# More idle-time identity products on TensorE, and GpSimd's power in two halves

## The chip, the cores and the metric

One core of one Trainium2 chip. The metric is the device time of one execution in microseconds; shown are the median of three runs and one execution that was profiled. The engines are TensorE (PE in the rows; PEld is its weight load), VectorE (DVE), ScalarE (ACT), GpSimd (POOL) and SyncE (SP), which issues the DMAs. Each engine works through its own list of instructions and waits for the others by semaphores.

## The reference, cut to what matters

The input is 8 batches of 512 tokens with 128 features. Each batch goes through six blocks, each behind a layer norm without weights:

```python
x = L0_attn_x                                    # 8 x 512 x 128
x = x + 0.5 * _L0_ffn_ref(_layernorm(x), ...)    # low rank: U1, V1, gelu, U2, V2
x = x + _L0_attn_ref(_layernorm(x), ...)         # 16 heads of 8, causal softmax, a layer norm inside
x = x + 0.5 * _L0_ffn_ref(_layernorm(x), ...)
x = x + 0.5 * _L1_ffn_ref(_layernorm(x), ...)    # shared expert and 8 routed ones, top 2
x = x + _L1_attn_ref(_layernorm(x), ...)         # Taylor feature map, num / den
x = x + 0.5 * _L1_ffn_ref(_layernorm(x), ...)

def _layernorm(x, axis=-1, eps=1e-05):
    m = jnp.mean(x, axis=axis, keepdims=True)
    v = jnp.var(x, axis=axis, keepdims=True)
    return (x - m) / jnp.sqrt(v + eps)
```

## The kernel before

A batch lies in SBUF as 128 partitions x 4 tiles (NT) x 128 features. Its work is cut into two halves: A is the first three blocks (low rank, softmax attention, low rank), B the last three (experts, Taylor attention, experts). Two sides run at once, left and right, each with its own region of SBUF and four banks of PSUM. The left side does A for batch after batch (stream A1) and B of the last (B1); the right side does A of one batch (A2), and then B for the others (B2). So in the steady state A of one batch runs beside B of an earlier one, and one turn of that takes about 180 us.

Each half is a list of named steps (ORDER_A, ORDER_B), the same for all engines. `stat` and `centre` are the layer norm on VectorE; `norm` (A) and `split` (B) transpose its result on TensorE. `low`, `up0` and `down0` are the low-rank block, `qkv0`, `pad0`, `max`, `shift`, `exp`, `pv0`, `turn` and `out0` the softmax attention: `max` forms scores for the row maxima, `shift` transposes the maxima, `exp` forms the scores again with the shift in an extra row. In B, `router`, `gate` and `expert` are the experts, `qk1`, `v1`, `pad1`, `sq`, `den`, `recip`, `num`, `scale` and `out1` the Taylor attention: `recip` inverts the denominators on VectorE, and `scale` spreads the reciprocals over the partitions by a product on TensorE.

The order in which an engine takes steps of the two sides is written out by hand, one letter (L or R) for each step and engine, in LOOP. It is the same before and after. So an engine that waits for data of one side holds up the other side's steps behind it.

TensorE's results go through a ring of PSUM banks, three in A and two in B. `fill` waits until the bank's last user has read it. Behind `fill`, and ahead of the wait for the step's data, several steps call `warm` (L1170), which looks up the stream, the turn and the step in the table WARM (L156) and runs that many 128x128 products of the identity with itself into the bank, which the step then overwrites. In the rows these products are L1173, two instructions each (fp32). The table has 26 entries with 144 products.

The layer norm goes over three engines. `stat` on VectorE makes means and variances of the four tiles (L909, L912). `ln_scale` on GpSimd adds epsilon (L710) and takes the power -0.5 (L712), each for all four tiles at once (128x4 elements). `centre` on VectorE (L920) waits for the power and does the four tiles one after the other, and then the transposes on TensorE (L1181) may start. Other lines in the rows: L1225 is `down0` behind the gelu, L1260 and L1262 `max`, L1408 `scale` behind `recip` (L1135), L988 `pad0`.

Of the kernel before, what the change touches and what calls it, by code (L numbers as in the profile page):

```python
# [33 lines left out]
ALU = mybir.AluOpType  # L34
# [5 lines left out]
NT = S // P  # L40
# [29 lines left out]
def segment(kt, head, heads):  # L70

    if kt == 0:
        return head * S
    if kt == 1:
        return (heads + head) * S
    if kt == 3:
        return (heads + head) * S + WIDTH[1]
    return 2 * heads * S + head * WIDTH[2]
# [64 lines left out]
def turns_of(body):  # L144
# [10 lines left out]

WARM = {  # L156
# [7 lines left out]
}  # L164

LOOP = {
# [247 lines left out]
def build_program(nc, x, w, cst, out):  # L414
    ctx = ExitStack()
    with ctx:  # L416
        def sb(name, shape, dt=F32):
            return ctx.enter_context(nc.sbuf_tensor(name, shape, dt))
# [16 lines left out]
        neghalf = sb("neghalf", [P, NT])  # L435
# [34 lines left out]
        def attention_stream(name, side):  # L470

            h = stream(name, side)
            new = h.region.take
            h.T, h.per, h.lns = TA, PERA, 4
            h.ring, h.pv = h.banks[0:3], h.banks[3]
            h.lnT = new([P, S])
            h.probs = new([P, 2, COLS0])
            h.hid0 = h.probs[:, 1, 0:NF * S].rearrange("p (f s) -> p f s", f=NF)
            p16 = h.probs[:, 1, NF * S:].bitcast(F16)
            h.q0h, h.q0l, h.k0h, h.k0l = (p16[:, i * S:(i + 1) * S] for i in range(4))  # L480
            h.kall = p16[:, 4 * S:(4 + NG) * S].rearrange("p (g s) -> p g s", g=NG)
            h.low = h.probs[:, 1, NF * S:NF * S + S // 2].bitcast(F16)
            h.mixed = h.probs[:, 0, 8 * S:9 * S]
            h.staging = h.probs[:, 0, :]
            h.q0a = new([P, NG, S], F16)
            h.kpad0 = new([P, H0, S], F16)
            h.vaug = new([P, NT, H0, HD0 + 1])
            h.bmax, h.rmax = new([P, NU0 * NT]), new([P, NT, H0])
            h.offs = new([GH, NG, S], F16)
            h.oT = new([P, 2, S])  # L490
            h.rden = new([P, NG, NT, GH, 1])
            h.attn = new([P, NT, D])
            h.qk0_laid = [sem(f"qk0_laid{g}_{name}") for g in range(NG)]
            h.offs_laid = [sem(f"offs_laid{g}_{name}") for g in range(NG)]
            h.low_hi = sem(f"low_hi_{name}")
            (h.kpad0_ready, h.rmax_ready, h.masked0, h.pv0_done, h.oT_ready) = (
                 sem(f"kpad0_ready_{name}"), sem(f"rmax_ready_{name}"), sem(f"masked0_{name}"),
             sem(f"pv0_done_{name}"), sem(f"oT_ready_{name}"))
            return h
# [45 lines left out]
        A1, A2 = attention_stream("A1", 0), attention_stream("A2", 1)  # L545
        B1, B2 = taylor_stream("B1", 0), taylor_stream("B2", 1)
# [39 lines left out]
        def run(eng, fns, engine):  # L586

            steps(fns, 0, "all", engine)
# [15 lines left out]
        def drained(h, it, step, unit):  # L604

            u = h.T[step, unit]
            return it * (h.per.act if u.engine == "act" else h.per.dve) + u.count
# [86 lines left out]
        @block.gpsimd  # L694
        def _(pool):
            for h in (A1, A2):
                pool.memset(h.vaug[:, :, :, HD0:HD0 + 1], 1.0).then_inc(setup, 1)
            pool.memset(neghalf[:, :], -0.5).then_inc(setup, 1)
            pool.memset(epsilon[:, :], LN_EPS).then_inc(setup, 1)
            for k in range(GP):  # L700
                if k:
                    pool.memset(column[:, k, 0:k], 0.0)
                pool.memset(column[:, k, k + 1:32], 0.0)
                last = pool.memset(column[:, k, k:k + 1], 1.0)
            last.then_inc(setup, 1)
            pool.wait_ge(setup, SETUP)

            def ln_scale(h, it, k, step):
                pool.wait_ge(h.mv_ready, it * h.lns + k + 1)
                pool.tensor_tensor(h.vare[:, :], h.mv[:, :, 1], epsilon[:, :], ALU.add).then_inc(h.vare_ready, 1)  # L710
                pool.wait_ge(h.vare_ready, it * h.lns + k + 1)
                pool.tensor_tensor(h.rstd[:, :], h.vare[:, :], neghalf[:, :], ALU.pow).then_inc(h.rstd_ready, 1)  # L712

            def mask(buf, heads, kt, fill=0.0):

                step = {0: S, 1: S, 3: S, 2: WIDTH[2]}[kt]
                s0 = segment(kt, 0, heads)
                v = bass.AP(buf.tensor, buf.offset + s0, [list(buf.ap[0]), [step, heads], [1, P]])
                return pool.affine_select(out=v, in_=v, compare_op=ALU.is_ge, fill=fill, base=0,  # L719
                                          pattern=[[0, heads], [1, P]], channel_multiplier=-1)  # L720

            def exp(h, it, n, step):
                g, u = divmod(n, NU0)
                if u in COMPLETE0:
                    pool.wait_ge(h.act, drained(h, it, step, "s"))
                for kt in COMPLETE0.get(u, ()):
                    mask(h.probs[:, g % 2, :], GH, kt).then_inc(h.masked0, 1)

            def sq(h, it, n, step):
                p, u = divmod(n, NU1)  # L730
                if u in COMPLETE1:
                    k = p * NC + list(COMPLETE1).index(u)
                    pool.wait_ge(h.act, drained(h, it, step, "s"))
                    for kt in COMPLETE1[u]:
                        last = mask(h.wts[:, p % 2, :], 2, kt, -1.0)
                    last.then_inc(h.cut1, 1)
                    pool.wait_ge(h.cut1, it * NPAIR * NC + k + 1)
                    v = h.wts[:, p % 2, (u // 2 * 2) * S:(u + 1) * S]
                    pool.tensor_scalar(v, v, 1.0, 1.0, ALU.mult, ALU.add).then_inc(h.masked1, 1)  # L739

            run(pool, dict(stat=ln_scale, exp=exp, sq=sq), "pool")

# [118 lines left out]
        def _(dve):  # L862
            passed = Passed(dve)
# [51 lines left out]
            def centre(h, it, k, step):  # L915

                src = h.attn if h in (A1, A2) and k == 2 else h.x
                passed.wait_ge(h.rstd_ready, it * h.lns + k + 1)
                for t in range(NT):
                    last = dve.tensor_scalar(h.ln[:, t, :], src[:, t, :], h.mv[:, t, 0:1], h.rstd[:, t:t + 1],  # L920
                                             ALU.subtract, ALU.mult)
                last.then_inc(h.ln_ready, 1)
# [219 lines left out]
            def out1(h, it, n, step):  # L1142
                ps = full(passed, h, it, step, "y")
                if n:
                    passed.wait_ge(h.dve, drained(h, it, f"out1 {n - 1}", "y"))
                dve.tensor_tensor(h.x[:, :, :].rearrange("p t d -> p (t d)"), ps[:, :],
                                  h.x[:, :, :].rearrange("p t d -> p (t d)"), ALU.add).then_inc(h.dve, 1)

            fns = dict(stat=stat, centre=centre, split=split, low=low, down0=down0, qkv0=qkv0, pad0=pad0, pv0=pv0, turn=turn,
                       out0=out0, take=take, route=route, gate=gate, expert=expert, qk1=qk1, pad1=pad1, recip=recip,  # L1150
                       scale=scale, out1=out1)
# [323 lines left out]
```

## Time and profile before

| what | before |
|---|---|
| median of 3 runs | 1472.24 us (1469.65 to 1478.45) |
| profiled execution, its own time | 1475.7 us |
| its span, first to last instruction | 1474.0 us |
| TensorE busy | 1260.9 us |
| VectorE busy | 950.3 us |
| ScalarE busy | 724.7 us |
| GpSimd busy | 420.0 us |
| mean granted clock of TensorE | 0.953 |

A row of the timeline has start, length, engine, line, operation, output and inputs, count, and in brackets the idle time of the engine just before it and what ended that.
### The profile page before, as it was taken

How to read it: one execution, taken by the hardware profiler on the slowest of the kernel's cores; microseconds unless marked ns; L12 is line 12 of the kernel's file. 1: busy time of each engine (PE TensorE's matmuls, PEld its weight loads, DVE VectorE, ACT ScalarE, POOL GpSimd, SP SyncE). 2: the span in 40 equal slices, each digit the busy share in tenths (PEclk: the TensorE clock that was granted, in tenths of full speed). 3: DMA queues.
4: the chain of work that ended last, by engine and by line, in shares of the span. 5: the costliest groups of instructions: out<-in, count | busy, mean ns of one | idle time of the engine just before them, and what ended most of it. 6: DMA issues, size and time to landing. Idle time of an engine off the chain costs nothing. (4 is left out here: it accounts for less than half of the span.)

```text
span 1474.0 us, 27223 instructions
## 1 busy us (share of the span) xinstructions
PE 1260.9 (86%) x10352; PEld 733.0 (50%) x10352; DVE 950.3 (64%) x2923; ACT 724.7 (49%) x1245; POOL 420.0 (28%) x707
## 2 busy tenths in 40 slices
PE   5598778988788887998789987888888988889998
PEld 3254454446544465444554445544555434653456
DVE  6986487446983479634896448863488645874267
ACT  3166436644366444664346543565434654456543
POOL 1023102640026400263003630035300362016730
PEclk9799899999999999999999999899998999999999
DMA  3100001000010000100101000010010100011000
GB/s 118 43 2 1 8 22 44 1 8 16 8 52 1 8 22 9 44 1 8 29 2 45 1 8 23 4 48 1 8 30 1 44 2 1 1 51 44 2 1 15
DMA packets 37203, 28.78 MB, mean 20 GB/s; under 512 B 7960, under 2 KB 36304, under 8 KB 37072
## 3 DMA queue, kind: packets, MB, share of 16 engines
q1 hardware_dynamic: 37072, 27.04, 6.8%
q8 instruction: 82, 1.34, 0.4%
q14 instruction: 49, 0.40, 0.1%
HBM read 5.90 MB, written 2.10 MB: 5 GB/s over the span
## 5 line engine op out<-in xcount | busy, mean ns | idle before, releaser
L998 DVE TENSOR_REDUCE left<-bank 128x4 f32<-128x512 f32 x280 | 184.5, 682 | 28.5 <-PE bank L1262 26.7
L849 ACT ACTIVATE right<-bank 128x512 f32<-128x512 f32 x280 | 158.4, 596 | 89.0 <-PE bank L1372 80.3
L805 ACT ACTIVATE left<-bank 128x512 f32<-128x512 f32 x280 | 160.1, 598 | 82.8 <-PE bank L1283 81.3
L719 POOL TENSOR_SCALAR_AFFINE_SELECT left<-left 128x512 f32<-128x512 f32 (+1 forms) x144 | 82.8, 591 | 338.8 <-ACT left L805 303.3
L1196 PE MATMUL bank<-right,pairs 128*128 128x512 f16 x588 | 161.9, 398 | 11.9 <-DVE right L1077 5.8
L739 POOL TENSOR_SCALAR right<-right 128x1024 f32<-128x1024 f32 x168 | 153.0, 911 | 14.7
L1260 PE MATMUL bank<-left 128*128 128x512 f16 (+1 forms) x448 | 120.8, 319 | 34.5 <-DVE left L998 19.6
L719 POOL TENSOR_SCALAR_AFFINE_SELECT right<-right 128x256 f32<-128x256 f32 (+1 forms) x240 | 99.6, 427 | 161.0 <-ACT right L849 150.9
L1098 DVE SCALAR_TENSOR_TENSOR right<-bank,right 128x128 f32<-128x128 f32 x448 | 125.8, 342 | 11.8 <-PE bank L1348 6.9
L1398 PE MATMUL bank<-right 128*32 128x256 f32 (+3 forms) x1792 | 133.1, 435 | 0.0
L1348 PE MATMUL bank<-ew,right 128*128 128x128 f32 x896 | 120.5, 278 | 8.8 <-DVE right L1087 6.2
L1348 PEld LDWEIGHTS bank<-ew,right 128*128 128x128 f32 x896 | 114.1, 191 | 27.6 <-DVE right L1087 12.9
L1283 PE MATMUL bank<-left 128*128 128x512 f16 (+1 forms) x448 | 104.8, 307 | 23.5 <-DVE left L998 17.9
L824 ACT ACTIVATE right<-bank 128x512 f32<-128x512 f32 x112 | 66.1, 597 | 108.9 <-PE bank L1196 108.1
L710 POOL TENSOR_TENSOR right<-right,epsilon 128x4 f32<-128x4 f32 x25 | 5.4, 215 | 376.8 <-DVE right L912 376.8
L1372 PE MATMUL bank<-right 96*128 96x512 f16 x448 | 99.9, 307 | 4.3 <-ACT right L849 3.0
L1262 PE MATMUL bank<-negmask,identb 128*128 128x128 bf16 x512 | 100.1, 229 | 0.0
L1196 PEld LDWEIGHTS bank<-right,pairs 128*128 128x128 f16 x588 | 53.3, 102 | 74.2 <-DVE right L1108 12.4
L1398 PEld LDWEIGHTS bank<-right 128*32 128x32 f32 x1792 | 53.9, 109 | 64.8 <-issue 61.3
L1260 PEld LDWEIGHTS bank<-left 128*128 128x128 f16 x448 | 45.6, 102 | 76.2 <-DVE left L998 25.1
L1385 PE MATMUL bank<-right,column 128*32 128x256 f32 (+3 forms) x896 | 75.8, 448 | 1.2 <-POOL right L739 1.1
L1015 DVE COPY left<-bank 128x512 f32<-128x512 f32 x28 | 19.3, 689 | 84.4 <-PE bank L1294 84.4
(276 smaller groups left out, 2254.6 us busy)
## 6 DMA issues: line engine op xcount, KB each, us to landing
right<-right SPq DMA_DIRECT2D x168, 64.0 KB, 2.0
left<-left SPq DMA_DIRECT2D x168, 32.0 KB, 1.8
left<-x_dram SPq DMA_DIRECT2D x7, 256.0 KB, 2.8
out_dram<-right SPq DMA_DIRECT2D x7, 256.0 KB, 2.3
left<-left SPq DMA_DIRECT2D x24, 64.0 KB, 2.0
right<-right SPq DMA_DIRECT2D x24, 32.0 KB, 1.9
wo<-wo_dram SPq DMA_DIRECT2D x1, 512.0 KB, 3.6
ew<-ew_dram SPq DMA_DIRECT2D x1, 512.0 KB, 4.7
```

The lines of the kernel that those rows point to most:

```text
L719: return pool.affine_select(out=v, in_=v, compare_op=ALU.is_ge, fill=fill, base=0, pattern=[[0, heads], [1, P]], channel_multiplier=-1)
L739: pool.tensor_scalar(v, v, 1.0, 1.0, ALU.mult, ALU.add).then_inc(h.masked1, 1)
L805: act.activation(h.probs[:, g % 2, u * S:(u + 1) * S], ps[:, :], ACT.Exp).then_inc(h.act, 1)
L849: act.activation(h.wts[:, p % 2, u * S:(u + 1) * S], ps[:, :], ACT.Square, bias=1.0, scale=FEAT ** -0.5).then_inc(h.act, 1)
L998: dve.tensor_reduce(h.bmax[:, u * NT:(u + 1) * NT], ps[:, :].rearrange("p (b k) -> p b k", k=P), AX.X, ALU.max).then_inc(h.dve, 1)
L1098: last = dve.scalar_tensor_tensor(out=dst[:, t, :], in0=ps[:, t * P:(t + 1) * P], scalar=h.comb[:, t, e:e + 1], in1=h.acc[:, t, :], op0=AL ...
L1196: done = mm(out, left, right, start=first, stop=last)
L1260: mm(ps[:, c0:c0 + n_keys], h.q0a[:, g, qt * P:(qt + 1) * P], h.kpad0[:, g * GH + j, 0:n_keys], start=True, stop=False)
L1262: last = mm(ps[:, c0 + n_keys - P:c0 + n_keys], identb[:, :], negmask[:, :], start=False, stop=True)
L1283: last = mm(ps[:, c0:c0 + WIDTH[kt]], h.kpad0[:, g * GH + j, kt * P:(kt + 1) * P], h.q0a[:, g, kt * P:S], start=True, stop=True)
L1348: last = mm(ps[:, t * P:(t + 1) * P], h.hexp[:, e % 2, t * P:(t + 1) * P], ew2[:, e, :], start=True, stop=True)
L1398: last = mm(h.num[HD1 * j + c:HD1 * j + c + 32, kt * P:S], h.v1[:, kt, hd * HD1 + c:hd * HD1 + c + 32], h.wts[:, p % 2, c0:c0 + WIDTH[kt]] ...
```

## The change

Two things change. The table WARM has 63 entries with 401 products instead of 26 with 144: three entries grow (`norm 0` and `max 0` of A1's turn 1, `split 0` of B2's turn 5), and 37 are new. And `ln_scale` takes the power in two instructions of two tiles each, with one count of the semaphore behind each; `centre` waits for the first half ahead of tile 0 and for the second ahead of tile 2.

```diff
 WARM = {
     ("A1", 0, "up0 1"): 6, ("A2", 0, "down0 0"): 8, ("A1", 0, "low 1"): 6, ("A2", 0, "out0"): 4,
-    ("A1", 0, "down0 2"): 4, ("A1", 1, "norm 0"): 12, ("A1", 1, "low 0"): 4, ("A2", 0, "down0 3"): 4,
-    ("A1", 1, "max 0"): 12, ("B2", 0, "split 2"): 2, ("B2", 0, "router 1"): 6, ("A1", 2, "exp 0"): 2,
+    ("A1", 0, "down0 2"): 4, ("A1", 1, "norm 0"): 19, ("A1", 1, "low 0"): 4, ("A2", 0, "down0 3"): 4,
+    ("A1", 1, "max 0"): 28, ("B2", 0, "split 2"): 2, ("B2", 0, "router 1"): 6, ("A1", 2, "exp 0"): 2,
     ("B2", 1, "split 2"): 2, ("B2", 1, "router 1"): 4, ("B2", 2, "split 0"): 4, ("A1", 3, "up0 1"): 2,
     ("A1", 3, "shift 0"): 2, ("B2", 2, "router 1"): 6, ("B2", 3, "split 0"): 8, ("A1", 4, "up0 1"): 2,
-    ("B2", 3, "scale 4"): 4, ("B2", 3, "router 1"): 6, ("B2", 4, "router 1"): 4, ("B2", 5, "split 0"): 8,
-    ("A1", 6, "down0 0"): 6, ("B2", 6, "split 0"): 16,
+    ("B2", 3, "scale 4"): 4, ("B2", 3, "router 1"): 6, ("B2", 4, "router 1"): 4, ("B2", 5, "split 0"): 15,
+    ("A1", 6, "down0 0"): 6, ("B2", 6, "split 0"): 16, ("A1", 0, "down0 0"): 3, ("A1", 0, "max 0"): 16,
+    ("A1", 0, "shift 0"): 12, ("A2", 0, "max 0"): 5, ("A1", 0, "exp 0"): 11, ("A2", 0, "norm 2"): 5,
+    ("A1", 1, "down0 0"): 3, ("A1", 1, "norm 1"): 3, ("B2", 0, "router 0"): 6, ("B2", 0, "scale 0"): 8,
+    ("B2", 0, "scale 4"): 5, ("A1", 2, "down0 0"): 5, ("A1", 2, "norm 1"): 7, ("A1", 2, "shift 0"): 6,
+    ("B2", 1, "scale 0"): 8, ("A1", 2, "norm 2"): 3, ("B2", 1, "scale 4"): 5, ("A1", 3, "down0 0"): 5,
+    ("A1", 3, "norm 1"): 7, ("B2", 2, "scale 0"): 8, ("B2", 2, "scale 4"): 6, ("A1", 4, "down0 0"): 5,
+    ("A1", 4, "norm 1"): 7, ("B2", 3, "scale 0"): 7, ("A1", 5, "down0 0"): 5, ("B2", 3, "split 2"): 4,
+    ("A1", 5, "norm 1"): 6, ("B2", 4, "split 0"): 5, ("B2", 4, "scale 0"): 10, ("B2", 4, "scale 4"): 6,
+    ("A1", 6, "norm 1"): 7, ("A1", 6, "shift 0"): 3, ("B2", 5, "scale 0"): 6, ("A1", 6, "down0 2"): 4,
+    ("B1", 0, "split 0"): 3, ("B2", 6, "split 1"): 7, ("B1", 0, "scale 0"): 5,
 }
...
                 pool.wait_ge(h.vare_ready, it * h.lns + k + 1)
-                pool.tensor_tensor(h.rstd[:, :], h.vare[:, :], neghalf[:, :], ALU.pow).then_inc(h.rstd_ready, 1)
+                for t in range(0, NT, 2):
+                    pool.tensor_tensor(h.rstd[:, t:t + 2], h.vare[:, t:t + 2], neghalf[:, t:t + 2], ALU.pow)\
+                        .then_inc(h.rstd_ready, 1)
...
                 src = h.attn if h in (A1, A2) and k == 2 else h.x
-                passed.wait_ge(h.rstd_ready, it * h.lns + k + 1)
                 for t in range(NT):
+                    passed.wait_ge(h.rstd_ready, (it * h.lns + k) * 2 + t // 2 + 1)
                     last = dve.tensor_scalar(h.ln[:, t, :], src[:, t, :], h.mv[:, t, 0:1], h.rstd[:, t:t + 1],
                                              ALU.subtract, ALU.mult)
                 last.then_inc(h.ln_ready, 1)
```

## Rows read from the trace of the kernel before

**Rows 1.** The page's busy time of each engine, and the core's span and clock.

```profile
PE 1260.9 (86%) x10352; PEld 733.0 (50%) x10352; DVE 950.3 (64%) x2923; ACT 724.7 (49%) x1245; POOL 420.0 (28%) x707
...
core 0: 1474.0 us, clock 0.953
```

**Rows 2.** Whom TensorE waits for: us in total, times, longest us.

```profile
PE bank L1408 <- DVE right L1135: 21.4, 12, 3.0
PE bank L1181 <- DVE left L920: 21.3, 23, 2.2
...
PE bank L1181 <- DVE right L920: 13.4, 15, 2.0
```

**Rows 3.** The timeline of TensorE at `max 0` of A1's turn 1.

```profile
184.62 2.84 PE L1173 MATMUL bank<-ident 128*128 128x128 f32 x24
191.89 0.61 PE L1260 MATMUL bank<-left 128*128 128x512 f16 x1 [4.43 <-DVE left L988]
```

**Rows 4.** Stretches around it: length, then PE, PEld, DVE, ACT, POOL busy, PEclk, DMA.

```profile
188.20:191.66 3.46, 0.00 (x0) 0.00 (x0) 2.06 (x9) 0.00 (x0) 0.00 (x0) 1.00 0.18 50
191.66:195.07 3.41, 3.18 (x15) 1.62 (x16) 2.48 (x6) 0.00 (x0) 0.00 (x0) 0.50 0.20 55
```

**Rows 5.** Stretches at clock 0.50 behind places that get products: first, last, sum of 19.

```profile
44.88:51.71 6.83, 3.76 (x16) 1.59 (x16) 6.58 (x17) 0.00 (x0) 0.00 (x0) 0.50 0.18 50
...
1109.84:1113.25 3.41, 3.41 (x24) 1.59 (x22) 2.99 (x8) 1.41 (x4) 0.00 (x0) 0.50 0.03 6
sum 85.31, PE 76.55 PEld 41.96 DVE 46.67 ACT 26.26 POOL 7.59; mean PE 4.03 PEld 2.21 DVE 2.46 ACT 1.38 POOL 0.40
```

**Rows 6.** The other stretches at clock 0.50: the sum of 11.

```profile
sum 54.61, PE 47.38 PEld 26.83 DVE 35.79 ACT 22.29 POOL 6.76; mean PE 4.31 PEld 2.44 DVE 3.25 ACT 2.03 POOL 0.61
```

**Rows 7.** The timeline of TensorE, identity products in a stretch at clock 0.50.

```profile
557.96 2.02 PE L1173 MATMUL bank<-ident 128*128 128x128 f32 x8
```

**Rows 8.** The first and the last of 40 waits that get more products, timeline of TensorE.

```profile
25.12 1.06 PE L1225 MATMUL bank<-left,u 128*32 128x512 f32 x8 [1.00 <-ACT left L780]
...
1358.86 0.38 PE L1408 MATMUL bank<-left,spread 128*128 128x512 bf16 x1 [1.40 <-DVE left L1135]
```

**Rows 9.** The timeline of one layer norm, from the power to the transposes (A1's turn 3).

```profile
528.95 1.01 POOL L712 TENSOR_TENSOR left<-left,neghalf 128x4 f32<-128x4 f32 x1
529.99 1.12 DVE L920 TENSOR_SCALAR left<-left 128x128 f32<-128x128 f32 x4 [1.40 <-POOL left L712]
...
531.17 0.66 PE L1181 MATMUL bank<-ident,left 128*128 128x128 f32 x4 [1.94 <-DVE left L920]
```

**Rows 10.** Stretches from `scale 0` to `scale 4` of B2's turns 0 to 4.

```profile
294.29:330.94 36.65, 32.16 (x290) 16.91 (x291) 15.18 (x43) 16.04 (x27) 16.41 (x28) 0.91 0.03 8
475.63:511.68 36.05, 31.11 (x290) 16.40 (x291) 15.34 (x43) 16.64 (x28) 16.36 (x28) 0.95 0.03 8
656.78:692.32 35.54, 31.27 (x291) 16.47 (x291) 14.95 (x44) 16.15 (x27) 15.07 (x25) 0.95 0.03 9
836.66:872.29 35.63, 33.89 (x298) 18.06 (x299) 14.80 (x43) 16.06 (x27) 15.22 (x25) 0.90 0.03 8
1021.18:1057.75 36.57, 32.41 (x290) 17.28 (x291) 14.79 (x43) 15.94 (x27) 15.18 (x25) 0.91 0.03 8
```

**Rows 11.** Two whole turns, from `split 0` of B2 to the next one's.

```profile
197.65:379.79 182.14, 157.19 (x1271) 90.06 (x1269) 115.03 (x362) 91.58 (x156) 52.42 (x86) 0.93 0.06 17
379.79:559.77 179.98, 155.38 (x1284) 91.56 (x1285) 118.62 (x365) 90.50 (x155) 52.27 (x86) 0.96 0.07 17
```

**Rows 12.** GpSimd's groups: busy us, mean ns of one, idle before.

```profile
L712 POOL TENSOR_TENSOR left<-left,neghalf 128x4 f32<-128x4 f32 x31 | 31.3, 1010 | 2.4
...
L710 POOL TENSOR_TENSOR left<-left,epsilon 128x4 f32<-128x4 f32 x31 | 6.6, 213 | 127.2 <-DVE left L912 127.1
```

**Rows 13.** Whom VectorE waits for: us in total, times, longest us.

```profile
DVE left L920 <- POOL left L712: 22.3, 17, 2.7
...
DVE right L920 <- POOL right L712: 15.5, 18, 1.4
```

## The prediction

> **What bounds the kernel now.** I read the page first. TensorE is busy 1260.9 us of a span of 1474.0, VectorE 950.3, ScalarE 724.7, GpSimd 420.0 [rows 1]. So TensorE sets the pace, and there are two ways to gain on it: its 213 us of idle time (1474.0 - 1260.9), and its clock. The mean granted clock is 0.953 [rows 1]. The clock has two levels, 1.2 and 2.4 GHz (0.50 and 1.00 in the rows), so the lower one held for (1 - 0.953) x 2 x 1474 = 139 us.
>
> Next comes the list of whom TensorE waits for [rows 2]. Its longest entries aren't long single waits but the same short ones in every turn: `scale` (L1408) waits for the reciprocal of the denominators, 21.4 us in 12 waits, and the transposes of `norm` and `split` (L1181) wait for `centre` (L920), 21.3 and 13.4 us in 38 waits. They are dependence waits: TensorE makes something, another engine works on it, and TensorE's queue stands behind a step that needs it. The reader is to see that work put ahead of such a wait costs nothing as long as it ends before the data comes.
>
> Then the timeline at one such wait, beside the clock of the stretches around it [rows 3, 4]. At 184.62 us twelve identity products run, and then TensorE does nothing for 4.43 us until the padded keys are ready. In the stretch 188.20 to 191.66 it is idle throughout at a granted clock of 1.00. In the next one, 191.66 to 195.07, it works for 3.18 us at 0.50, and only then gets 1.00 again. So a long or repeated idle stretch is paid twice: once as idle, and once more as slow work after it.
>
> I then took every stretch with a granted clock of 0.50 and looked at what TensorE did before it. There are thirty. Ahead of 19 of them (85.31 us) lies a wait in front of which the change puts products [rows 5]; ahead of the other 11 (54.61 us) it puts none [rows 6].
>
> **The change, step by step.**
>
> *The products' own time.* A product is two instructions. 24 of them take 2.84 us at full clock [rows 3], 0.237 us a product; 8 take 2.02 us at the lower level [rows 7], 0.505 us a product. 257 x 0.237 = 61 us of added work. The 40 places that get more products have idle waits of 75.4 us in the before run, of which the first is 1.00 us (3 products, 0.71 us) and the last 1.40 us (5 products, 1.19 us) [rows 8]. At `norm 1`, the wait is 1.94 us [rows 9] and gets 7 products, 1.66 us. So at full clock the products end ahead of the data, and their cover is the wait itself: cost 0. If that cover is gone, the whole 61 us lie on TensorE's path. At the lower level they need 257 x 0.505 = 130 us, 54 more than the waits hold.
>
> *The clock.* If the products keep the clock up, the 19 stretches of [rows 5] run at full clock. Their TensorE work is 76.55 us, and at double speed 38 us of it go: 0.45 us for each us of half clock. That is the upper bound. The lower bound is 0, because other engines may be what the stretch waits for: in 44.88 to 51.71 VectorE is busy 6.58 of 6.83 us, so a faster TensorE would only wait for it. What is really carried I read from repeated work. The stretch from `scale 0` to `scale 4` occurs in five turns [rows 10]: 36.65, 35.63 and 36.57 us at clocks of 0.90 to 0.91 (mean 36.28), 36.05 and 35.54 at 0.95 (mean 35.80). At a clock of c, half clock lasts 2 x (1 - c) of the stretch: about 6.8 us against 3.6. So 0.48 us are won per 3.2 us, 0.15 of it. For a whole turn, 182.14 us at 0.93 stand against 179.98 at 0.96 [rows 11]: 2.16 us for 25.5 - 14.4 = 11.1 us, 0.19. I take 0.2, on the side of the whole turn, as it holds what is given back later: 85.3 x 0.2 = **-17 us** (bounds 0 and -38).
>
> The Trainium skill has a rule against this part: the page "TensorE: Matmul & The Clock Gate", section Part 1 on the clock gate, says that for modelling the ramp penalty is under 1% of a typical kernel's span. By that sentence the clock could give at most 14.7 us here; with the 139 us above it would be 28 us at 0.2, so the trace speaks for more, but only the result can tell. It is weighed as part of the second rival.
>
> *The power in two halves.* After `bn_aggr` GpSimd adds epsilon (0.213 us mean for 128x4) and takes the power (1.010 us for 128x4) [rows 12]. `centre` starts 0.03 us behind the power, runs 1.12 us for four tiles, and the transposes start 0.06 us behind its end [rows 9]. VectorE stood idle for the power 22.3 us in 17 waits and 15.5 in 18 [rows 13]: 35 waits, 1.08 us each. Now `centre` starts after the first half. No row shows a power on 128x2, so its price is bounded: not under the 0.2 us of the addition (then it would be nearly all fixed cost of an instruction), and not over the 1.01 us of the whole. The addition is the nearest row: same form, same size, so what it takes is the fixed part and the other 0.8 us belong to the power of four columns. I take 0.2 + 0.4 = 0.6. The first half then ends 0.4 us sooner; the second ends at 1.2 us, when `centre` is at 0.6 + 2 x 0.28 = 1.16, so it waits hardly at all. Gain 0.4 us x 35 = 14 us at most, and only where TensorE waits for `centre` and nothing else. Those 38 waits hold 34.7 us [rows 2], 0.9 each, but in several VectorE had other work between and idled for little. I take under half: **-6 us** (bounds -14 and, with a fixed 1.0 us, +18: the second half would come at 2.02, `centre` would end at 2.02 + 0.56 instead of 2.13, 0.45 to 0.5 later, 35 times). The added instruction's time on GpSimd is hidden: it is busy 420 of 1474 us [rows 1].
>
> *Both together.* Where the wait for `centre` shrinks from 1.94 to 1.54 us, 7 products (1.66 us) end 0.1 us late. Some 16 of the 40 places are of this kind: **+2 us**.
>
> Sum: -17 - 6 + 2 = -21 us. The profiled execution took 1475.7 us with a span of 1474.0; it lies 3.5 us above the median of 1472.24. 1475.7 - 21 = 1454.7, a ratio of 0.986; of the median, **1451 us**. The main case's own range is 1438 to 1462.
>
> **The rivals.**
>
> 1. *The clock rises and little of it arrives* (chance 0.25). TensorE's work gets shorter and its next wait longer, as the chains it waits for are paced by VectorE and ScalarE; the waits of [rows 2] are of that kind, and five turns show only 0.15 [rows 10]. At 0.05, 4 us, and half of the power's gain, 3 us: 1475.7 - 7, or 1465 beside the median. The skill's rule of under 1% would end here or just above.
> 2. *The power has a fixed price* (0.09). +18 against the clock's -17: 1473. Against it stands the 0.2 us of the addition.
> 3. *All of it arrives* (0.08). -38 - 12: 1475.7 - 50, or 1422. For it: TensorE is 90% busy in the 19 stretches (76.55 of 85.31). Against it: [rows 10, 11].
> 4. *The products themselves run at the lower level* (0.04), and this ends on the other side. A place loses as soon as a product takes over 75.4 / 257 = 0.29 us. If the clock is low when they start and they don't lift it, each takes 0.505 us, and 54 us of waits are overrun: 1475.7 + 54 - 6, or about 1520. Against it: before the idle stretch of [rows 4] the clock is 1.00 and the products there run at 0.237 us.
>
> **How the numbers follow.** The main case has 0.54. The predicted time is its own, 1451. Some 1% is what a measurement of this kernel can tell from no change: 1457.5 to 1487. Of the main case about 0.48 lies below 1457.5; with rival 3, faster is 0.56. Rivals 1 and 2 and the upper end of the main case lie within 1%: 0.40. Rival 4 is slower, 0.04. The range goes from 1430 (below the main case, short of rival 3) to 1473 (rivals 1 and 2); it leaves out rivals 3 and 4 and some of the edges, about 0.17.
>
> **What would show it.** *Clock:* the mean granted clock should be 0.97 to 0.98, and the stretches at 0.50 that follow `scale 0`, `scale 4`, `down0 0`, `norm 1` and `max 0` gone. The eleven others should be there, perhaps at other times. *Products:* TensorE's busy time up by 61 us less what the clock gives back (about 38), waits of L1408 for VectorE down from 21.4 us to a few. A wait that is now shorter than its products shows as an instruction that starts behind them without idle time. *Power:* 112 instructions of 128x2 at about 0.6 us, VectorE's wait for GpSimd at L920 down from 37.8 to about 24 us. At 1.0 us rival 2 holds. *Carry:* if the clock rises as said and the turns still take 180 us, it is rival 1. The prediction is wrong in its foundation if the clock doesn't rise, that is, if half-clock stretches come back elsewhere as fast as they go.

## The result, and the profile after

The changed kernel takes 1451.32 us (median of 4 runs, 1447.42 to 1455.21) beside 1474.58 us of the kernel before (its three runs and a fourth). The ratio is 0.984, with a 95% interval of 0.981 to 0.987: 1.6% faster, 23 us. The profiled execution took 1447.42 us, span 1445.7. TensorE's busy time and the clock, from the page and the core's span:

```profile
PE 1288.7 (89%) x10866; PEld 777.4 (54%) x10866; DVE 945.8 (65%) x2923; ACT 724.3 (50%) x1245; POOL 439.5 (30%) x763
...
core 0: 1445.7 us, clock 0.980
```

Against [rows 1], TensorE is busy 27.8 us more: the products are in, and the rest of its work became shorter. The granted clock went from 0.953 to 0.980; the four runs have 0.973 to 0.980, mean 0.9765. Half clock lasts 2 x (1 - clock) of the time, so it fell from 139 us in the profiled run before to 58 us in this one, and to 68 us in the mean of the four runs.

Whom TensorE waits for (us in total, times, longest us); `scale` is now L1419, the transposes L1192, the identity products L1184 and `max` L1271:

```profile
PE bank L1192 <- DVE left L931: 10.1, 21, 1.2
...
PE bank L1192 <- DVE right L931: 5.1, 10, 1.6
...
PE bank L1419 <- DVE right L1146: 3.6, 9, 0.6
```

Where [rows 2] had 21.4, 21.3 and 13.4 us, there are 3.6, 10.1 and 5.1. The timeline of TensorE at two of the places shows why. Rows of the timeline have start, length, engine, line, operation, count and the idle time just before:

```profile
183.24 6.42 PE L1184 MATMUL bank<-ident 128*128 128x128 f32 x56
190.50 0.39 PE L1271 MATMUL bank<-left 128*128 128x512 f16 x1 [0.84 <-DVE left L999]
...
469.08 2.05 PE L1184 MATMUL bank<-ident 128*128 128x128 f32 x16
471.71 0.39 PE L1419 MATMUL bank<-right,spread 128*128 128x512 bf16 x1 [0.58 <-DVE right L1146]
```

The 4.43 us of [rows 3] are 0.84 now, and `scale` waits 0.58 us behind eight products. The first real product behind them takes 0.39 us, where it took 0.61 in the stretch of half clock that followed the idle time before. In all, the 40 places hold 11.9 us of idle time instead of 75.4; in 26 of them the data still come after the products.

The stretches at a granted clock of 0.50 that are left, 12 of them (length, busy time and count of each engine, PEclk, DMA); the first rows shown are two of a kind that returns in nearly every turn:

```profile
227.51:234.34 6.83, 6.00 (x22) 2.64 (x20) 3.80 (x11) 2.92 (x6) 0.81 (x2) 0.50 0.00 1
370.87:377.70 6.83, 4.44 (x34) 3.22 (x35) 6.47 (x19) 2.08 (x3) 1.75 (x3) 0.50 0.00 1
...
sum 58.01, PE 49.13 PEld 31.19 DVE 44.23 ACT 17.56 POOL 8.11; mean PE 4.09 PEld 2.60 DVE 3.69 ACT 1.46 POOL 0.68
```

What TensorE did at those two, in its timeline:

```profile
226.65 0.39 PE L1294 MATMUL bank<-left 128*128 128x384 f16 x2 [1.99 <-DVE left L1009]
...
373.06 0.50 PE L1271 MATMUL bank<-left 128*128 128x384 f16 x1 [4.61 <-DVE left L1009]
```

They are `exp 4` and `max 6` of A1. Both wait in `fill`, for a bank that VectorE's row maxima (L1009) have not read yet. `warm` stands behind `fill`, and `max` and `exp` call it only in the first of every ten steps, so nothing in the table could have filled these waits. Of the twelve stretches, eleven stand behind a `max 6` or an `exp 4` and one behind `shift 0` of A1's turn 5. Three of the twelve (13.65 us) are at places behind which the kernel before had none. No stretch of half clock is left behind `scale`, `down0`, `norm 1` or `max 0`.

The layer norm: GpSimd's groups (busy us, mean ns of one, idle before), whom VectorE waits for, and the timeline of `norm 1` in A1's turn 3:

```profile
L722 POOL TENSOR_TENSOR left<-left,neghalf 128x2 f32<-128x2 f32 x62 | 42.3, 701 | 2.4
...
L719 POOL TENSOR_TENSOR left<-left,epsilon 128x4 f32<-128x4 f32 x31 | 6.6, 212 | 111.0 <-DVE left L923 110.9
```

```profile
DVE left L931 <- POOL left L722: 18.5, 18, 2.8
...
DVE right L931 <- POOL right L722: 10.1, 10, 1.1
```

```profile
521.91 1.36 POOL L722 TENSOR_TENSOR left<-left,neghalf 128x2 f32<-128x2 f32 x2
522.02 1.72 PE L1184 MATMUL bank<-ident 128*128 128x128 f32 x14
522.64 1.28 DVE L931 TENSOR_SCALAR left<-left 128x128 f32<-128x128 f32 x4 [1.08 <-POOL left L722]
...
523.97 0.66 PE L1192 MATMUL bank<-ident,left 128*128 128x128 f32 x4 [0.23 <-DVE left L931]
```

A half of the power takes 0.70 us against 1.01 for the whole [rows 12]. VectorE idles 1.08 us where it idled 1.40 [rows 9], and 28.6 us in 28 waits where it was 37.8 in 35 [rows 13]. `centre` itself got 0.16 us longer (1.28 against 1.12), because the second half comes late for its third tile: it ends at 521.91 + 1.36 = 523.27, when the first two tiles are done (522.64 + 2 x 0.28 = 523.20).

Last, the stretches from `scale 0` to `scale 4` in B2's turns 0, 1 and 4, and two whole turns from `split 0` to the next one's:

```profile
294.29:328.40 34.11, 31.12 (x300) 16.80 (x301) 14.44 (x43) 16.04 (x27) 17.06 (x30) 1.00 0.03 9
471.71:505.91 34.20, 31.84 (x306) 17.56 (x307) 14.69 (x43) 16.64 (x28) 17.04 (x30) 1.00 0.03 9
...
999.22:1033.50 34.28, 31.70 (x302) 16.91 (x303) 14.02 (x43) 15.94 (x27) 15.85 (x27) 1.00 0.03 9
```

```profile
196.00:374.08 178.08, 158.12 (x1333) 93.61 (x1330) 114.75 (x362) 91.58 (x156) 54.94 (x93) 0.97 0.07 17
374.08:552.38 178.30, 161.55 (x1353) 97.17 (x1353) 118.13 (x365) 90.52 (x155) 54.56 (x93) 0.97 0.07 18
```

At full clock throughout, the first kind takes 34.1 to 34.3 us, 1.9 to 2.5 less than the same turns in [rows 10], by both parts of the change together (turns 2 and 3 took 33.26 and 31.61 us against 35.54 and 35.63); the turns take 178.1 and 178.3 instead of 182.1 and 180.0 [rows 11].

### The profile page after: what moved, and what is told of

It is laid out like the page before. It is cut to its first block and busy times, and to the rows that moved or that the text cites. A ratio compares the mean times of both kernels' runs of the same rounds, so it can differ in the third digit from the quotient of the medians.

```text
span 1445.7 us, 28280 instructions
## 1 busy us (share of the span) xinstructions
PE 1288.7 (89%) x10866; PEld 777.4 (54%) x10866; DVE 945.8 (65%) x2923; ACT 724.3 (50%) x1245; POOL 439.5 (30%) x763
## 3 DMA queue, kind: packets, MB, share of 16 engines
q8 instruction: 86, 1.41, 0.4%
## 5 line engine op out<-in xcount | busy, mean ns | idle before, releaser
L1009 DVE TENSOR_REDUCE left<-bank 128x4 f32<-128x512 f32 x280 | 184.6, 683 | 29.8 <-PE bank L1273 28.0
L1207 PE MATMUL bank<-right,pairs 128*128 128x512 f16 x588 | 158.0, 391 | 13.6 <-DVE right L1088 6.7
L750 POOL TENSOR_SCALAR right<-right 128x1024 f32<-128x1024 f32 x168 | 152.6, 908 | 14.7
L1271 PE MATMUL bank<-left 128*128 128x512 f16 (+1 forms) x448 | 118.2, 312 | 29.5 <-DVE left L1009 21.6
L1294 PE MATMUL bank<-left 128*128 128x512 f16 (+1 forms) x448 | 104.5, 306 | 17.8 <-DVE left L1009 13.8
L1184 PE MATMUL bank<-ident 128*128 128x128 f32 x802 | 107.4, 287 | 2.5 <-DVE left L1009 1.3
L1184 PEld LDWEIGHTS bank<-ident 128*128 128x128 f32 x802 | 100.1, 199 | 17.3 <-issue 9.3
L1271 PEld LDWEIGHTS bank<-left 128*128 128x128 f16 x448 | 45.0, 100 | 69.8 <-DVE left L1009 27.2
```

The costliest lines, as they stand in the source:

```text
L1009: dve.tensor_reduce(h.bmax[:, u * NT:(u + 1) * NT], ps[:, :].rearrange("p (b k) -> p b k", k=P), AX.X, ALU.max).then_inc(h.dve, 1)
L1184: mm(ps[:, 0:P], ident[:, :], ident[:, :], start=True, stop=True)
L1207: done = mm(out, left, right, start=first, stop=last)
L1271: mm(ps[:, c0:c0 + n_keys], h.q0a[:, g, qt * P:(qt + 1) * P], h.kpad0[:, g * GH + j, 0:n_keys], start=True, stop=False)
L1294: last = mm(ps[:, c0:c0 + WIDTH[kt]], h.kpad0[:, g * GH + j, kt * P:(kt + 1) * P], h.q0a[:, g, kt * P:S], start=True, stop=True)
```

## The experiments

The theory was the forecast's: two separate gains, the larger from the clock, at about 0.2 us for each us of half clock that goes, the smaller from the layer norm. The first rival was that the layer norm made the gain and the clock little; the second, that what the products do has nothing to do with the clock. Ratios are against the kernel before on the same chip; the mean half clock of a kernel is worked out from the clocks of its runs. In the diffs, `-` and `+` are against the kernel that the text names.

### One part at a time

`e1_products_only` is the kernel before with the new table; `e2_power_only` is the changed kernel with the old table.

```diff
 # e1, against the kernel before: the table of 401 products, ln_scale and centre as they were
 # e2, against the changed kernel: the table of 144 products, ln_scale and centre changed
```

> The 257 products without the split power (one instruction of 128x4, as before). Clock theory: the granted clock rises as in the changed kernel, 0.953 to about 0.975, some 65 to 70 us of half clock less, and each is worth 0.2 to 0.35 us: 14 to 24 us faster, about 1455. Rival, that the shorter way through the layer norm made the gain: the clock rises and the time stays within 5 us of before.

> The split power with the 144 products of before. A half takes 0.70 us in the changed kernel against 1.01 for the whole, so centre may start 0.3 us sooner. Clock theory: clock as before (0.95), 25 places with up to 0.3 us, some of it carried: 2 to 6 us faster, about 1470. Rival, that the layer norm made the gain: about 1453.

The products alone: 1461.94 us, ratio 0.9906 (0.9875 to 0.9938), so 13.8 us, at a mean clock of 0.976. The power alone: 1462.11 us, ratio 0.9908 (0.9871 to 0.9944), 13.5 us (11.5 by the means of the runs), at 0.954. The two parts are worth about the same. The theory was right that the clock gains and that both gains are separate; the size of the power was off by a factor of two, and neither rival holds. Their sum, 27 us, is not told apart from the 23 us of both together by these intervals. In `e2` VectorE waits for GpSimd like this:

```profile
DVE left L922 <- POOL left L713: 17.3, 15, 2.7
...
DVE right L922 <- POOL right L713: 10.1, 10, 1.1
```

That is 27.4 us against 37.8 [rows 13]: 10.4 us less idle time of VectorE, for 8 to 19 us less time of the kernel. So all of it arrived, as far as this interval tells.

### More and fewer products

`e3_no_products` empties the table of the kernel before. `e4_more_products` adds 108 products to the changed kernel, at the waits that its profile above shows as left over. They run ahead of `fill`, into the bank of the accumulator `pv`, which is free at that time.

```diff
 # e3, against the kernel before
-WARM = {...}
+WARM = {}
 # e4, against the changed kernel
+EARLY = {("A1", 1, "max 6"): 5, ("A1", 1, "exp 4"): 7, ("A1", 2, "max 6"): 16, ("A1", 2, "exp 4"): 7, ...}
+            def early(h, it, step):
+                for _ in range(EARLY.get((h.name, it, step), 0)):
+                    mm(h.pv[:, 0:P], ident[:, :], ident[:, :], start=True, stop=True)
 # in max, exp and shift
+                early(h, it, step)
                 ps = fill(passed, h, it, step, "s")
```

> The kernel before with the table empty: none of its 144 products either. Clock theory: some 25 to 50 us more at half clock (0.935 to 0.945), and 0.2 to 0.35 us for each: 5 to 17 us slower, about 1485. Rival, that the clock is paid only in stretches that wait for other engines: within 4 us of before, or faster by what the old products cost.

> The changed kernel with 108 more products in front of waits where it still falls to half clock: max 6 and exp 4 of A1 (and shift 0, max 9 once), run into the accumulator bank before the wait for the ring's bank. Clock theory: half clock from about 66 us to 20, clock 0.99, at 0.2 to 0.35 us for each 9 to 16 us faster than the changed kernel, about 1438. Rival: these stretches are paced by VectorE's maxima, so the clock rises to 0.99 and the time stays at 1451.

Without any products: 1485.18 us, ratio 1.0065 (1.0035 to 1.0096), clock 0.928. With 108 more: 1440.46 us, ratio 0.9769 (0.9733 to 0.9804), clock 0.9945. So `e4` beats both kernels, by 2.3% and, through the kernel before, by 0.7% against the changed one (0.2 to 1.2% by the two intervals). The doses together (means of the runs, half clock from the mean clock):

| kernel | clock | half clock, us | time, us | us of time per us of half clock |
|---|---|---|---|---|
| no products (e3) | 0.928 | 213 | 1484.8 | |
| before, 144 products | 0.951 | 146 | 1473.6 | 0.17, from e3 |
| products only, 401 (e1) | 0.976 | 70 | 1459.4 | 0.19, from before |
| changed kernel, 401 | 0.977 | 68 | 1451.3 | |
| 509 products (e4) | 0.995 | 16 | 1440.1 | 0.21, from the changed kernel |

Three doses of products, of different places, give 0.17 to 0.21 net of what the products cost. By the intervals of the ratios each of them could be some 0.1 from that, so that they agree so closely is partly luck; that none is 0 holds for each. The rival that the stretches left over are paced by VectorE and carry nothing is out: `e4` filled most of those.

### Products of 8 columns

`e6_thin_products` is the changed kernel with the added products cut to 8 columns. They are as many instructions with the same weight loads.

```diff
-                for _ in range(WARM.get((h.name, it, step), 0)):
-                    mm(ps[:, 0:P], ident[:, :], ident[:, :], start=True, stop=True)
+                for i in range(WARM.get((h.name, it, step), 0)):
+                    cols = P if i < WIDE.get((h.name, it, step), 0) else 8    # WIDE: the old table
+                    mm(ps[:, 0:cols], ident[:, :], ident[:, 0:cols], start=True, stop=True)
```

> The changed kernel, but the 257 added products have 8 columns instead of 128: as many instructions and weight loads at the same places, with a sixteenth of the columns. If the products work by keeping TensorE's array at work, the clock stays at 0.95 and the time at that of the split power alone, about 1462. If instructions or weight loads in the wait are what counts, the clock rises to 0.975 and the time is 1451 or less.

1467.42 us, ratio 0.9967 (0.9948 to 0.9987), mean clock 0.953. The identity products take as long in all as in the changed kernel; here are their groups, of this kernel and then of the changed one (busy us, mean ns):

```profile
L1194 PE MATMUL bank<-ident 128*128 128x8 f32 (+1 forms) x802 | 110.4, 279 | 2.8 <-DVE left L1018 1.6 <-ACT left L800 1.1
```

```profile
L1184 PE MATMUL bank<-ident 128*128 128x128 f32 x802 | 107.4, 287 | 2.5 <-DVE left L1009 1.3 <-ACT left L791 1.1
```

So the waits are filled just as long, and the clock stays where it was without the added products. The thin ones alone, by their form:

```profile
L1194 PE MATMUL bank<-ident 128*128 128x8 f32 x514 | 70.2, 270 | 2.3 <-DVE left L1018 1.6 <-ACT left L800 0.7
```

The gain goes too, and a little more: the kernel is some 5 us above `e2` by the means (1467.5 and 1462.1, on different chips) and 9 by the ratios. What costs that is not shown. This was the run that tells the second rival apart: filling the wait is no gain in itself, and the wide products gain by the clock. From `e6` to the changed kernel 138 - 68 = 70 us of half clock go and the ratio falls from 0.9967 to 0.9841, 18.6 us (13 to 24): some 0.26 for each us.

### The price of the layer norm's way

`e5_power_late` is `e2` with `centre` waiting for both halves first. `e7_more_power_whole` is `e4` with the power in one instruction.

```diff
 # e5, against e2
-                    passed.wait_ge(h.rstd_ready, (it * h.lns + k) * 2 + t // 2 + 1)
+                    passed.wait_ge(h.rstd_ready, (it * h.lns + k) * 2 + 2)
 # e7, against e4: ln_scale and centre as in the kernel before
```

> The power in two halves with the 144 products of before, but centre waits for both halves ahead of its first tile: the way through the layer norm is 2 x 0.70 - 1.01 = 0.4 us longer than before instead of 0.3 shorter. If the power's gain is the length of that way (13.6 us for 0.3 us), the time goes up by about as much for 0.4 us: 10 to 18 us, about 1487. If the way is mostly hidden behind other work, as the forecast's 6 us took it: 3 to 8 us slower, about 1479. If the gain of the split came from something else: within 3 us of before.

> The kernel with 108 more products (clock 0.994, 1440 us), with the power in one instruction again. If the split power gains apart from the clock: 9 to 14 us slower than that one, about 1451. If at full clock the products fill the time that the split saves, 0 to 4 us slower, about 1442.

`e5`: 1485.61 us, ratio 1.0093 (1.0059 to 1.0128), 13.7 us slower for 2 x 0.70 - 1.01 = 0.39 us more in each norm. Whom VectorE waits for in it:

```profile
DVE left L922 <- POOL left L713: 29.3, 19, 3.4
...
DVE right L922 <- POOL right L713: 21.4, 18, 1.7
```

50.7 us in 37 waits, 12.9 more than before, and the time went up by 13.7. With `e2` (10.4 less, 13.5 down) this says that, for the power's length, an us which VectorE waits at `centre` is about an us of the kernel. `e7`: 1452.89 us, ratio 0.9862 (0.9827 to 0.9898) against 0.9769 of `e4`: 13.7 us slower (6 to 21) at a clock of 0.993 as well, with 39.2 us of VectorE's wait for GpSimd against 28.1. So the split power keeps its worth where the clock is almost always full; nothing here ties it to the clock.

### Too many products

`e8_half_more` has half as many again of the added products at each of the 40 places.

> The changed kernel with half as many again of the added products at each of the 40 places (126 more, 30 us at 0.237 us). The places have 11.9 us of wait left, so at least 18 us of it is late work on TensorE. If late products lie on the path: 8 to 18 us slower than the changed kernel, less 2 to 4 us for a higher clock, about 1460. If what is late is taken up by later waits: 1449 to 1452, with a clock of 0.98 to 0.985.

1456.09 us, ratio 0.9896 (0.9864 to 0.9929), clock 0.979: 5 us above the changed kernel (8 by the ratios, intervals overlapping). 30 us of products went into 11.9 us of waits; of the 18 us or more that came late, 5 to 8 show in the time (1 to 15 by the two intervals). Lateness is paid, but less than by its length.

### The whole layer norm in halves

`e9_norm_in_halves` lets `stat` and epsilon go in halves too, on top of `e4`.

```diff
-                for t in range(NT):
-                    last = dve.bn_stats(h.stats[:, t, :], src[:, t, :])
-                h.chain.then(last)
...
+                for two in ((0, 1), (2, 3)):
+                    for t in two:
+                        last = dve.bn_stats(h.stats[:, t, :], src[:, t, :])
+                    h.chain.then(last)
+                    for t in two:
+                        last = dve.bn_aggr(h.mv[:, t, :], h.stats[:, t, :])
+                    last.then_inc(h.mv_ready, 1)
 # and ln_scale: epsilon and power of one half, then of the other
```

> The kernel with 108 more products (1440 us), with the whole layer norm in two halves: stat, epsilon, power and centre take tiles 0 and 1 and then 2 and 3, so that GpSimd starts about 0.6 us sooner and ends about 0.35 us sooner, for one more instruction of 0.2 us on GpSimd and one more wait on VectorE. If every us of the layer norm's way counts 35 times, as the late and the whole power showed: 8 to 13 us faster than that kernel, about 1430. If the second half's power becomes the bound and only the first tiles come sooner: 1436 to 1441. If VectorE's added waits cost as much as the way saves: 1440 to 1445.

1438.0 us, ratio 0.9764 (0.9738 to 0.9791), against 0.9769 of `e4`: no gain that these runs can tell. The timeline of one norm in it:

```profile
514.20 0.48 DVE L930 BATCH_NORM_STATS2 left<-left 128x6 f32<-128x128 f32 x2
514.71 0.25 DVE L933 BATCH_NORM_AGGREGATE left<-left 128x2 f32<-128x6 f32 x2
514.87 0.45 DVE L930 BATCH_NORM_STATS2 left<-left 128x6 f32<-128x128 f32 x2
515.04 0.20 POOL L728 TENSOR_TENSOR left<-left,epsilon 128x2 f32<-128x2 f32 x1 [4.57 <-DVE left L933]
515.31 0.69 POOL L731 TENSOR_TENSOR left<-left,neghalf 128x2 f32<-128x2 f32 x1
515.36 0.25 DVE L933 BATCH_NORM_AGGREGATE left<-left 128x2 f32<-128x6 f32 x2
515.96 0.20 POOL L728 TENSOR_TENSOR left<-left,epsilon 128x2 f32<-128x2 f32 x1
516.04 0.60 DVE L941 TENSOR_SCALAR left<-left 128x128 f32<-128x128 f32 x2 [0.43 <-POOL left L731]
516.24 0.69 POOL L731 TENSOR_TENSOR left<-left,neghalf 128x2 f32<-128x2 f32 x1
516.97 0.60 DVE L941 TENSOR_SCALAR left<-left 128x128 f32<-128x128 f32 x2 [0.33 <-POOL left L731]
```

GpSimd is now the line of this norm: 0.20 + 0.69 twice, from 515.04 to 516.93, and both halves of `centre` wait for it. From the first statistics to the end of `centre` it is 3.37 us; in the changed kernel it was 3.64 (520.28 to 523.92). At a price of 35 waits that should have been worth 9 us, and it wasn't seen. VectorE's part up to the last means takes 1.41 us instead of 1.27 (520.28 to 521.55), in each of 56 norms, also in those that wait for nothing: up to 8 us of VectorE. Whom VectorE waits for, in `e4` and then in `e9`:

```profile
DVE left L938 <- POOL left L729: 18.0, 17, 2.7
...
DVE right L938 <- POOL right L729: 10.1, 10, 1.1
```

```profile
DVE left L941 <- POOL left L731: 13.7, 30, 2.4
...
DVE right L941 <- POOL right L731: 6.5, 18, 0.4
```

The wait did fall, from 28.1 to 20.2 us, and the time with it by 0.7 us (by the ratios, 7 at the edge of the intervals) to 2.7 (by the means). So the rule of `e2`, `e5` and `e7` does not seem to hold here. VectorE is busy 948.7 us in `e9` against 943.4 in `e4`. That this took the gain back is argued, not shown; it stays open.

## Why the prediction was right

The time was forecast as 1451 us and measured as 1451.32; the range was 1430 to 1473. So close a hit is luck: the forecast took 21 us from a median of 1472.24, and with the fourth run that median is 1474.58. Point by point:

- **The bound and the places.** Right. Products in front of dependence waits found room: idle time at the 40 places went from 75.4 to 11.9 us, and `scale`'s wait from 21.4 to 3.6 us.
- **The clock's level.** Forecast 0.97 to 0.98, measured 0.973 to 0.980. The stretches behind places with products went, and what is left stands mostly at `exp 4` and `max 6`, in front of which the table had nothing. `e6` shows that the wide products, not the filling, raised it.
- **What the clock is worth.** Forecast 0.2 us per us, taken between 0.15 and 0.45 "on the side of the whole turn". Three doses gave 0.17, 0.19 and 0.21, products' cost included. That the forecast's 0.2 fell among them is partly luck: it came from two turns, and their clocks have two decimals, so that the 11.1 us of half clock between them could be 7.5 or 14.7. The -17 us stand against 13.8 us measured with the products alone (9 to 18). Half the distance is that 76 us of half clock went on average instead of 85; the trace has new stretches at places that had been quiet. The price before the products' own cost is rather 0.26 (`e6` against the changed kernel).
- **The products' own cost.** Forecast 0, and 2 us where `centre` comes sooner. `e6` puts it at 5 to 9 us for products that don't raise the clock; in the changed kernel it is not measured by itself. No row shows the 2 us: the places that wait for `centre` are 14 and not 16, and at 10 of them TensorE still idles behind its products (0.23 us at `norm 1` above). `e8` shows that products too many cost 5 to 8 us where 18 us came late.
- **The power.** This is the term that was mis-sized: -6 us forecast, -13.5 measured (8 to 19). Two estimates failed in opposite directions. The price of a half: 0.60 us was put together as the addition's 0.2 plus half of the rest; it is 0.70, so that the split saves 0.31 us and not 0.4. And the carry: "I take under half" of 35 waits, on the ground that VectorE had other work between. `e2`, `e5` and `e7` show that the time moved about as far as VectorE's wait at `centre`: +12.9 us of wait gave +13.7, 10.4 us less gave -13.5, and 11.1 more gave +13.7. The 35 waits of [rows 13] were the right count for this step, 35 x 0.31 = 11 us, and needed no discount. The likely reason is that the waits were counted when VectorE was idle already, so that the work in between had been taken out once. `e9`, where 7.9 us less wait gave some 1 to 3 us, speaks against a rule for every change of the norm.
- **The sum.** -21 us forecast, -23 measured (19 to 28). It came out right because the clock's term was some 3 us too large, the power's some 7 too small, and both together may lose a few us against the parts (27 against 23, within the intervals). That the errors cancelled is luck.
- **The rivals.** The one with little carry is out by the three doses. From `e3` to `e7`, which both have the power whole, the ratio falls from 1.0065 to 0.9862: the products, from none to 509, were worth 30 us, 2%. The sentence of the Trainium skill ("TensorE: Matmul & The Clock Gate", Part 1) that the ramp penalty is under 1% of a typical span does not hold for this kernel, by that measurement. The fixed price of the power is half true: by the two sizes, 0.40 us are fixed and 0.15 us are for each column. That all arrives is out by the same doses. The rival of products at the lower level was not met: even in `e6`, where they don't raise the clock, an instruction of a thin product takes 0.270 us in the mean, near the 0.275 of each of the 24 in [rows 3] at full clock and far from the 0.42 of each of the 8 in [rows 7], and the loss against `e2` is 5 to 9 us, not 54.

## What to carry to other kernels

Where an engine's clock falls after idle time, list the stretches at the lower level, and for each the wait ahead of it: the waits that could be filled with 128-column products of no use were worth about a fifth of the half clock that went here, and one that stands ahead of the filling (a wait for the bank) needs another place to write. An idle wait of the next engine in a dependence chain, counted where that engine is idle, was worth about its whole length in three experiments: don't discount it a second time without a reason. In a fourth, which cut the work of that engine into smaller pieces to shorten the wait, hardly any of it was seen. And a filler that is too long costs: size it from the wait in the profile.

## What the runs showed of the hardware

GpSimd's power on 128 partitions takes 1.01 us for four columns and 0.70 for two: by these two sizes 0.40 us for the instruction and 0.15 for each column, against 0.20 us for an addition, of two columns or of four. An identity product of fp32 takes nearly the same time with 8 columns as with 128 (eight thin ones in 1.95 us, eight wide ones in 2.05), so its 128 columns aren't what sets its length here; but only the kernel with the wide ones had the higher clock (0.977 against 0.953).

```profile
656.04 1.95 PE L1194 MATMUL bank<-ident 128*128 128x8 f32 x16
```
